# Attention scores in three PSUM areas of two banks in place of two of three, with exponentials of 1024 columns in place of 1536

## The reference

```python
# layer 0, for each image
qkv = einsum('oc,bchw->bohw', w_qkv, x)            # 3 x 256 channels
q, k, v = split(qkv)                               # 8 heads of d = 32
scores = einsum('bhdi,bhdj->bhij', q, k) / sqrt(d) # 4096 x 4096 per head
out = einsum('bhij,bhdj->bhdi', softmax(scores), v)
x = einsum('oc,bchw->bohw', w_proj, out) + x
# layer 1: theta (64 channels, 4096 positions) against phi (64 channels,
# pooled to 1024 positions), softmax over 1024, times g (256 channels, pooled),
# a 1x1 convolution with a batch norm, and + x
```

## Time and profile before

| | |
|---|---|
| median of 3 runs | 2495.67 us (2495.59 to 2498.33) |
| profiled execution, its own time | 2489.87 us |
| profiled execution, its span | 2487.6 us |
| mean granted TensorE clock | 0.997 |
| TensorE matmuls busy | 2429.1 us (98%), 33064 instructions |
| ScalarE busy | 2221.6 us (89%) |
| VectorE busy | 2140.5 us (86%) |
| four attention stages, in us from the start | 43.6 to 507.0, 545.8 to 1009.4, 1275.7 to 1739.3, 1778.1 to 2241.7 |

### The profile page before, as it was taken

One profiled execution on the slowest core, in us unless ns is written; L12 is line 12 of the kernel. 1 busy time (PEld: TensorE's weight loads), 2 busy tenths in 40 slices (PEclk: granted clock), 3 DMA queues, 4 the chain that ended last, 5 costly groups with the idle time before them and its releaser, 6 DMA issues.

```text
span 2487.6 us, 74166 instructions
## 1 busy us (share of the span) xinstructions
PE 2429.1 (98%) x33064; PEld 1082.3 (44%) x33064; DVE 2140.5 (86%) x1354; ACT 2221.6 (89%) x1826; POOL 456.8 (18%) x652
## 2 busy tenths in 40 slices
PE   8999999999999999999999999999999999999997
PEld 4444444444444444344454444444444444443443
DVE  6999999969999999895579999999799999998854
ACT  7999999989999999566489999999899999994763
POOL 0222222202222222110012222222022222220200
PEclk9999999999999999999999999999999999999999
DMA  8777777767777877502277777777677777874011
GB/s 245 162 157 161 160 158 162 153 179 159 160 158 157 163 158 152 157 1 77 80 204 159 162 156 161 156 159 152 184 157 160 161 158 158 163 154 122 1 64 40
DMA packets 150257, 359.98 MB, mean 145 GB/s; under 512 B 23088, under 2 KB 65392, under 8 KB 149680
## 3 DMA queue, kind: packets, MB, share of 16 engines
q0 software_dynamic: 73728, 268.47, 54.1%
q1 hardware_dynamic: 76208, 86.78, 11.3%
HBM read 52.63 MB, written 33.85 MB: 35 GB/s over the span
## 4 chain that ended last, share of the span: by engine, by line
PE 73%; ACT 16%; issue 4%; DVE 3%; SPq 2%; DMA 2%; ACTq 0%; POOL 0%; DVEq 0%
PE scores L528 27%; PE psOL L541 26%; ACT arena L610 15%; PE psOL L965 7%; PE scores L349 3%; DVE arena L659 2%; PE psOL L889 1%; PE scores L360 1%; PE scores L952 1%; PE scores L953 1%; PE scores L942 1%; SPq L1252 1%; PE scores L943 1%; DMA att_inv<-Ls 1%; PE psOL L512 1%
## 5 line engine op out<-in xcount | busy, mean ns | idle before, releaser
L610 ACT ACTIVATE arena<-scores 128x1536 f32<-128x1536 f32 x1368 | 1849.2, 1461 | 5.3 <-PE scores L528 2.8
L659 DVE TENSOR_TENSOR arena<-arena 128x2048 f32<-128x2048 f32 x732 | 1674.9, 2291 | 123.4 <-ACT arena L610 71.2
L528 PE MATMUL scores<-arena 96*32 96x512 f16 x16384 | 1125.0, 379 | 13.2 <-ACT arena L610 11.6
L541 PE MATMUL psOL<-arena 128*32 128x256 f32 (+1 forms) x13120 | 1105.4, 432 | 0.0
L528 PEld LDWEIGHTS scores<-arena 96*32 96x32 f16 x16384 | 399.2, 95 | 698.2 <-ACT arena L610 393.8
L688 POOL DMA_DIRECT2D arena<-arena x448 | 388.7, 894 | 1125.4 <-ACT arena L610 838.3
L541 PEld LDWEIGHTS psOL<-arena 128*32 128x32 f32 x13120 | 391.3, 110 | 341.9 <-issue 7.4
L965 PE MATMUL psOL<-arena 128*128 128x512 f16 x768 | 170.3, 379 | 0.0
L685 POOL DMA_DIRECT2D arena<-arena x64 | 35.3, 556 | 567.7 <-ACT arena L610 567.4
L1229 DVE SCALAR_TENSOR_TENSOR arena<-arena 128x1536 f16<-128x1536 f32 (+1 forms) x48 | 75.8, 1581 | 68.2 <-ACT arena L1075 62.6
L1068 ACT ACTIVATE arena<-scores 128x1536 f32<-128x1536 f32 (+1 forms) x48 | 62.5, 1302 | 73.6 <-PE scores L953 73.6
(11 more groups left out here) (119 smaller groups left out, 1164.7 us busy)
## 6 DMA issues: line engine op xcount, KB each, us to landing
arena<-arena POOLq DMA_DIRECT2D x512, 512.0 KB, 5.4
arena<-qk_parts SPq DMA_DIRECT2D x192, 128.0 KB, 3.8
qk_parts<-arena SPq DMA_DIRECT2D x32, 512.0 KB, 3.6
X<-in_x SPq DMA_DIRECT2D x16, 512.0 KB, 4.5
att_out<-arena SPq DMA_DIRECT2D x32, 256.0 KB, 3.7
arena<-att_out SPq DMA_DIRECT2D x16, 512.0 KB, 10.5
out<-arena SPq DMA_DIRECT2D x32, 256.0 KB, 2.0
arena<-att_inv SPq DMA_DIRECT2D x16, 256.0 KB
```

The costliest lines, as they stand in the source:

```text
L528: last = nc.tensor.matmul(bank[k % 2][m * D:(m + 1) * D, i * CH:(i + 1) * CH], KS[0:3 * D, h, j * 128 + m * D:j * 128 + (m + 1) * D], QS2[ ...
L541: last = nc.tensor.matmul(both(c)[h * D:(h + 1) * D, lo:hi], V[:, j, h * D:(h + 1) * D], P[:, r + h, lo:hi], start=(j == 0), stop=(j == JT ...
L610: nc.scalar.activation(P[:, u % RING:u % RING + size, :], bank[k % 2][:, 0:size * CH].rearrange("p (u n) -> p u n", n=CH), ACT.Exp, scale= ...
L659: nc.vector.tensor_tensor(new, old, P[:, r:r + G, :], ALU.add).then_inc(s_add, 1)
```

## The change

The group is cut from 3 units to 2, and the six banks of `scores6` are used as three areas of two banks in place of two areas of three. TensorE computes scores up to three groups ahead of the finished exponentials in place of two. The ACTIVATE has 1024 columns in place of 1536, so one attention has 512 groups in place of 342 (the last of which had one unit). SUMS_A and SUMS_D count steps; in units they stay where they were (8 x 3 = 12 x 2 = 24, 20 x 3 = 30 x 2 = 60). The rate of values becomes 68 x 2 / 128 = 1.06 halves a step. Nothing else changes: the same matmuls, adds and DMAs, the same ring of 36 units, and layer 1 keeps its own two areas of three banks.

```diff
-GROUP = 3
+GROUP = 2
+AREAS = 3
 RING = 36
...
-SUMS_A, SUMS_D, BEHIND = 8, 20, 2
+SUMS_A, SUMS_D, BEHIND = 12, 30, 2
...
+        def area(k):
+
+            return scores6[:, k % AREAS * GROUP * CH:(k % AREAS + 1) * GROUP * CH]
...
-                            last = nc.tensor.matmul(bank[k % 2][m * D:(m + 1) * D, i * CH:(i + 1) * CH],
+                            last = nc.tensor.matmul(area(k)[m * D:(m + 1) * D, i * CH:(i + 1) * CH],
...
-                scores(1)
+                for k in range(1, AREAS):
+                    scores(k)
                 for k in range(GROUPS):
                     pe.wait_ge(s_exp, k + 1)
-                    if k + 2 < GROUPS:
-                        scores(k + 2)
+                    if k + AREAS < GROUPS:
+                        scores(k + AREAS)
...
-                                         bank[k % 2][:, 0:size * CH].rearrange("p (u n) -> p u n", n=CH),
+                                         area(k)[:, 0:size * CH].rearrange("p (u n) -> p u n", n=CH),
```

## The result

The changed kernel takes 2518.19 us (median of 4 runs, 2515.68 to 2520.7), the kernel before 2495.63 (2491.12 to 2498.33 in its 4 runs beside them). The ratio is 1.009 (95% interval 1.0077 to 1.0102): slower by 0.9%, with 2520 forecast.

What follows compares the result with a forecast made beforehand. TensorE and ScalarE were taken as matched, with ScalarE the only bound after the change. 4 x 5.7 + 3 x 0.4 = +24 us on 2489.87 gives 2514, plus 5.8 to the median: 2520 us, range 2492 to 2535.

Steps and rivals of the forecast that it cites:

- Two engines matched within 1%, stalls invisible in the idle column: Attention, per chunk before the change: TensorE 57.0 us of work, ScalarE 56.7 at its own pace, 57.9 measured.
- the 9.2 us per attention: ScalarE's exponentials before the change: starts 1.357 us apart against 1.330 unhindered, read as waiting, 37 us in all.
- Three areas take the stalls away: Attention: scores ready up to three exponentials ahead should remove all stalls of 0.08 to 0.2 us, at most -9.2 per attention.
- Fixed part of an exponential: ScalarE: about 0.05 us fixed per exponential; 0.904 plus 0.012 gives a lasting pace of 0.916 us for 1024 columns.
- How it shows: Profile after: starts 0.916 us apart, durations above 1.1 that stay, TensorE's weight loads waiting for L616 in nearly every step.
- The sum: Per attention, first start to last end: 469.1 us in place of 463.4, so +5.7.
- The extra +0.4 at the start of each later attention: Attentions 2 to 4: about 0.6 us idle awaiting the second group's scores, less 0.22 for an earlier first exponential.
- The base: Whole kernel: profiled execution 2489.87 us, median of the runs 5.8 above it, a distance carried over to the forecast.
- A: Rival, no creep, no difference: lasting pace 0.904 us, stalls won eaten by more fixed parts; 2495.7 us, chance 0.20.
- B: Rival, faster: fixed part shrinks with scores ready early, pace below 0.89, TensorE the bound; 2473 us, chance 0.07.
- C: Rival, dearer fixed part: a 1024-column exponential costs 0.947 us like a copy; 2584 us, chance 0.06.
- D: Rival, stalls stay because average load causes them, not the two areas; 2530 us or so, chance 0.05.

Runs made afterwards that it cites:

- the run with less work on TensorE: The changed kernel with half of each value matmul's columns left out for key tiles 1 to 30: 2517.85 us, ratio 1.009.
- the two runs with less work on TensorE: Half of each value matmul's columns left out for key tiles 1 to 30, in the changed kernel (2517.85 us) and the kernel before (2474.84 us).

## Why the prediction was right, point by point

- **Two engines matched within 1%, stalls invisible in the idle column**: right. But the 9.2 us per attention counted as waiting held two things. About 4.1 us went with less work on TensorE (463.57 against 459.52). The other 5 stayed: ScalarE's own lag, which every stall before paid back.
- **Three areas take the stalls away**: wrong as written. I had forecast none, and the second attention has 37 long distances. What goes is the loss through uneven steps. The long distances left are the lag being paid, as the run with less work on TensorE shows: same time with 22 of them. The prediction did say that at some point the starts must follow the ends, but not by what: it is by these waits for scores, which themselves waited for a late end. With two areas of this width it would have been 62 us worse.
- **Fixed part of an exponential**: right, and the term that decided. I took 0.916 from the first nine durations and the 512-column row; the ends are 0.9167 apart, the mean of the starts 0.916. The fixed part is 0.063 us, 170 times more per attention is 10.7 us (10.3 between the two runs with less work on TensorE), against 4.1 won.
- **How it shows**: wrong. I expected starts 0.916 apart over long stretches and durations that rise above 1.1 us "and then stay". Starts are 0.904 apart and durations rise to 1.83. I thought the lag could hardly outgrow an instruction; it reached 0.8 us here and 1.7 us with 512 columns. TensorE's weight loads did not wait for L616 in nearly every step either: in the second attention it was 323 of 512 steps (104 us), against 242 of 342 (98 us) before.
- **The sum**: +5.7 us per attention was forecast. From the first start to the last end the first attention grew from 463.38 to 469.42, the second from 463.57 to 469.82, so +6.0 and +6.2. The extra +0.4 at the start of each later attention did not come. They are longer than the first by 0.4 now, but were by 0.2 before, and attentions 2 and 4 start 0.22 earlier, as forecast: from the start of the first to the start of the second the time grew by 5.8, from the third to the fourth by 6.0. So the sum was 0.3 us too low in each of the four attentions and 0.4 too high in each of the three later ones, and the two errors cancel. The range's upper end adds up to 2534, not 2535.
- **The base**: the forecast carried 5.8 us from the profiled execution to the median. After the change the profiled execution (2518.79) is near its median (2518.19), and it is the medians, 22.6 us apart, that come near the 24 forecast. Between the two profiled executions lie 28.9 us. That the forecast hit within 2 us is in part luck, since the executions of one kernel spread wider than that: the kernel before took 2492.4 to 2502.0 us in the 15 beside the last experiments.
- **Rivals**: A fell, since its pace of 0.904 is there in the starts and yet not the lasting one. B would have needed a pace below 0.902. C fell with the 0.917. It rested on the fixed part of a copy out of SBUF and on the Trainium skill, ScalarE: Activation LUTs, section What ACT_TABLE_LOAD costs, whose figures (186 ns less an overlap of 93) leave 93 ns per back-to-back ACTIVATE; these traces say 63 ns for a read out of PSUM with fp32 output, and the measurement decides. The page's 0.833 ns a column agrees with the 0.833 between the three sizes here. D fell with the run with less work on TensorE.

## What to carry to other kernels

Where two engines are matched, judge a producer of back-to-back instructions by the distance of its *ends*: the starts may look faster for dozens of instructions, and the idle column shows nothing. An instruction's fixed part should be measured at two sizes in the trace and multiplied by the new count before a finer tiling is tried; here 170 more instructions of 0.063 us cost more than all the stalls they could remove. If the aim is only to even out the partner's steps, cut the partner's work more finely instead.

## What the runs showed of the hardware

ACTIVATEs out of PSUM, issued back to back with fp32 output, start 0.478, 0.904 and 1.330 us apart for 512, 1024 and 1536 columns, but end 0.490, 0.917 and 1.343 apart. The recorded duration grows by 12 to 13 ns with each, up to 2.27 us for an instruction that lasts 0.59 alone, and nothing seen here but a wait brings it back. TensorE sees the late end: its scores start 0.05 us after it, at a duration of 1.19 us as at 1.96. It is not the function (Square does the same), not the signal (with every second one left out the ends stay 0.490 apart), not the width. VectorE's and the DMAs' additions are not needed for it either. In the first attention of the changed kernel it has begun before the first of VectorE's additions, and the first accumulating DMAs start at 49.8 us:

```profile
L616 ACT ACTIVATE arena<-scores x3: 1021/1036/1046, 44.8 to 46.6; 128x1024 f32<-128x1024 f32 x3
```

```profile
L665 DVE TENSOR_TENSOR arena<-arena x5: 2269/2293/2295, 49.7 to 59.3; 128x2048 f32<-128x2048 f32 x5
```

The cause of the lag stays open, and so does whether it needs a source in PSUM or an output in fp32: neither was tried. Nor was a run made with the other engines quiet. With a quarter less work on TensorE the lag still grew by 12 to 13 ns an exponential, but that the other engines' accesses have no part in it is not shown.
